# A two-layer perceiver block with int8-style feed-forward on one core: first loads reordered, last normalisation on POOL, float16 GELU inputs with an offset

## The reference

```python
x = x + xattn(layernorm(x), ctx, ctx, mask, Wq, Wk, Wv, Wo)   # 16 heads of 8, causal
x = x + attn(layernorm(x), Wq, Wk, Wv, Wo, Wd, Wuk, Wuv)       # 16 heads, scores clipped, times a decay
x = x + ffn(layernorm(x), w1, b1, w2, b2)
# ffn: each linear quantises its input and its weight by one scale for the whole tensor
s  = max(max(abs(v)), 1e-6) / 127
h  = gelu((round(x/sx) @ round(w1/sw).T + b1) * (sw*sx))
o  = (round(h/sh) @ round(w2/sw2).T + b2) * (sw2*sh)
```

## Time and profile before

| What | us |
|---|---|
| median of 3 runs | 324.59 |
| the profiled execution's own time | 324.61 |
| its span, first to last instruction | 322.8 |
| PE busy (share of the span) | 292.3 (91%) |
| DVE busy | 256.5 (79%) |
| ACT busy | 250.1 (77%) |
| POOL busy | 226.9 (70%) |
| mean granted PE clock | 0.974 |

### The profile page before, as it was taken

The page is one execution under the profiler, slowest core; times in us unless marked ns, Lnnn a source line. Parts: engine busy times, 40 slices in busy tenths (PEclk is TensorE's granted clock), DMA queues, the critical chain, the costliest instruction groups (busy, mean ns, idle before and its releaser), DMA issues.

```text
span 322.8 us, 13785 instructions
## 1 busy us (share of the span) xinstructions
PE 292.3 (91%) x5792; PEld 205.0 (64%) x5792; DVE 256.5 (79%) x561; ACT 250.1 (77%) x544; POOL 226.9 (70%) x176
## 2 busy tenths in 40 slices
PE   4796989999999999999999999999999998575884
PEld 3455757676767676867677777776667767321363
DVE  1486587899977887888788887878788998679883
ACT  3485795868687988787889898889877877499583
POOL 5177576874969697879999999999989970055000
PEclk9798999999999999999999999999999999759999
DMA  8999000000000000000000000000000000000027
GB/s 194 229 199 198 3 2 2 2 4 3 4 2 4 2 4 4 2 4 2 2 4 4 4 4 2 4 3 4 4 2 4 4 3 5 2 0 0 0 66 196
DMA packets 19102, 9.54 MB, mean 30 GB/s; under 512 B 5153, under 2 KB 18786, under 8 KB 19042
## 3 DMA queue, kind: packets, MB, share of 16 engines
q1 hardware_dynamic: 18322, 8.25, 12.0%
q10 hardware_dynamic: 720, 0.43, 0.6%
HBM read 6.57 MB, written 2.10 MB: 27 GB/s over the span
## 4 chain that ended last, share of the span: by engine, by line
PE 75%; ACT 14%; DVE 4%; issue 3%; DMA 1%; ACTq 1%; SPq 0%; DVEq 0%
PE ps L554 13%; PE ps L535 11%; PE ps L581 9%; PE ps L587 8%; PE ps L597 8%; PE ps L475 5%; ACT arena L860 4%; PE ps L459 4%; PE ps L468 4%; PE ps L552 4%; PE ps L566 3%; PE ps L645 2%; PE ps L441 2%; ACT arena L775 2%; DMA arena<-in_ctx 1%
## 5 line engine op out<-in xcount | busy, mean ns | idle before, releaser
L782 ACT ACTIVATE pt<-ps 128x512 f32<-128x512 f32 x128 | 75.9, 594 | 21.7 <-PE ps L554 20.7
L386 POOL TENSOR_TENSOR u<-u,mx 128x1024 f32<-128x1024 f32 x32 | 60.8, 1902 | 37.1 <-DVE mx L991 36.9
L378 POOL TENSOR_TENSOR ud<-u,con 128x1024 f32<-128x1024 f32 x31 | 73.5, 2372 | 1.9 <-DVE u L977 1.9
L972 DVE SCALAR_TENSOR_TENSOR u<-ps,rs,arena 128x1024 f32<-128x1024 f32 x32 | 41.0, 1282 | 20.3 <-PE ps L535 20.2
L535 PE MATMUL ps<-arena,qT 32*64 32x256 f32 x1024 | 44.2, 401 | 6.4 <-ACT arena L775 4.3
L977 DVE TENSOR_SCALAR u<-ps 128x1024 f32<-128x1024 f32 x32 | 39.0, 1220 | 12.5 <-PE ps L535 12.1
L581 PE MATMUL ps<-pt,vx 128*32 128x64 f32 x2048 | 41.0, 221 | 1.7 <-DVE oT L918 1.5
L581 PEld LDWEIGHTS ps<-pt,vx 128*32 128x32 f32 x2048 | 32.2, 110 | 14.8 <-issue 10.0
L587 PE MATMUL ps<-pt,con 128*32 128x128 f32 x1024 | 40.0, 275 | 0.0
L991 DVE TENSOR_REDUCE mx<-u 128x16 f32<-128x1024 f32 x32 | 38.7, 1210 | 0.1
L535 PEld LDWEIGHTS ps<-arena,qT 32*64 32x64 f32 x1024 | 14.9, 129 | 32.2 <-issue 22.5
(11 more groups left out here) (153 smaller groups left out, 568.2 us busy)
## 6 DMA issues: line engine op xcount, KB each, us to landing
out<-pt SPq DMA_DIRECT2D x8, 256.0 KB, 2.3
x<-in_x SPq DMA_DIRECT2D x4, 256.0 KB, 3.6
arena<-in_ctx SPq DMA_DIRECT2D x8, 128.0 KB, 4.1
x<-in_x SPq DMA_DIRECT2D x2, 512.0 KB, 7.0
arena<-in_ctx SPq DMA_DIRECT2D x4, 256.0 KB, 6.6
arena<-in_mask_BxS_if SPq DMA_DIRECT2D x2, 256.0 KB, 5.7
arena<-in_mask_BxS_if SPq DMA_DIRECT2D x4, 64.0 KB, 3.9
arena<-in_mask_BxS_if SPq DMA_DIRECT2D x2, 128.0 KB, 3.8
```

What stands on the lines that cost most here:

```text
L378: pool.tensor_tensor(dh, uh, decay.unsqueeze(1).to_broadcast([P, H, HALF]), ALU.mult)\
L386: pool.tensor_tensor(uh, uh, mx[:, n % 4, 0:count].unsqueeze(2).to_broadcast([P, count, HALF]), ALU.subtract)\
L782: act.activation(pt[:, n % 2, 4 * half:4 * half + 4].rearrange("p h n -> p (h n)"), ps[:, bank, :], ACT.Exp).then_inc(s["emptied"], 1)
L972: dve.scalar_tensor_tensor(by_head(u[:, n % UB]), sc, rs[:, 0, n:n + 1], mask[:, n].unsqueeze(1).to_broadcast([P, H, HALF]), ALU.mult, ALU ...
```

## The change

Six edits are in it.

Start: the context's first half is issued by ACT ahead of the identity, its second half by SP ahead of x; ACT's order is then identity, Wk, other constants, Wq, Wv. PE first runs 8 products on a zeroed tile `warm`, and the first pieces become c, x, k, cq, q.

Run-out: POOL normalises group 6 and three tiles of group 7; DVE normalises group 5 and tile 31 alone. The last tile's attention has a bank of its own (`num_den`), so it does not wait for the tile before it.

First maximum: its PE steps use bank 7 and stand ahead of the wait for the last copy. ACT loads the GELU table before its last two copies.

Up product: `x16` goes into PE as it is. `open_up` opens each pair of banks with w1 times -1536; the second pass into `xq` is gone. The first and the last GELU are halved.

Down product: POOL sums w2's four parts (`w2s`) in turns 30 and 31, so that `open_down` needs one product with `minus_off`, and the bias product moves into it, from the end of each group. Four groups are opened before the second maximum, the others between its steps and the first groups.

Rounding of the hidden values: ACT has groups 1, 3, 5, 7, POOL 2 and 6, DVE 0 (in halves) and 4.

```diff
-X_ACT = (1, 2, 3)
-X_POOL = 4
-H_ACT = (1, 2, 4, 5, 7)
-DVE_TAIL = (("a", 0), ("a", 3), ("f", 0), ("f", 1), ("a", 6)) + tuple(("f", g) for g in range(2, 8))
+WARM = 8
+X_ACT, X_DVE, X_POOL = (1,), (0, 2, 3), (4, 5, 6, 7)
+H_ACT, H_POOL = (1, 3, 5, 7), (2, 6)
+DVE_TAIL = (("a", 0), ("a", 4)) + tuple(("f", g) for g in range(8))
+GELUS = ((0, 0, 1), (0, 1, 2)) + tuple((k, 0, 2) for k in range(1, 15)) + ((15, 0, 1), (15, 1, 2))
...
-    pieces[-1] = [("x", 0), ("cq", 0), ("c", 0), ("q", 0), ("k", 0)]
+    pieces[-1] = [("c", 0), ("x", 0), ("k", 0), ("cq", 0), ("q", 0)]
...
+            def last_norm(g, tiles):
+
+                pool.wait_ge(RS[2], batch_of(2, tiles[-1]))
+                pool.wait_ge(s["filled"], gets_empty(("x3", g - 2)))
+                pool.wait_ge(s["amax_done"], g - 1)
+                for t in tiles:
+                    last = pool.tensor_scalar(xn3[:, g % 2, t % GT], x[:, t], mv[:, 2, t, 0:1], rs[:, 2, t:t + 1],
+                                              ALU.subtract, ALU.mult)
+                last.then_inc(s["xn3_pool"], 1)
...
+                if n == 30:
+                    pool.wait_ge(s["emptied"], gets_empty(("w2", 0)))
+                    pool.tensor_tensor(w2p[:, :, :], w2qT[:, 0:2], w2qT[:, 2:4], ALU.add).then_inc(s["w2_summed"], 1)
...
+            pool.wait_ge(s["hscale"], 2)
+            for g in H_POOL:
+                if g >= 6:
+                    pool.wait_ge(s["down_done"], g - 5)
+                pool.tensor_scalar(h16[g % 6], hidden[:, :, g * GT * P:(g + 1) * GT * P], scal[:, 19:20], ROUND16,
+                                   ALU.mult, ALU.add).then_inc(s["hr_done_pool"], 1)
...
+            def open_up(k):
+
+                for m in range(2):
+                    pe.matmul(ps[:, 2 * (k % 4) + m, :], w1qT[:, k % FC],
+                              minus_off[:, :].unsqueeze(1).to_broadcast([P, GT, P]), start=True, stop=False)
+
+            def open_down(g):
+
+                pe.matmul(ps[:, g, :], minus_off[:, :], w2s[:, :].unsqueeze(1).to_broadcast([P, GT, D]),
+                          start=True, stop=False)
+                pe.matmul(ps[:, g, :], ones_b[:, :], b2q[:, :].unsqueeze(1).to_broadcast([96, GT, D]),
+                          start=False, stop=False)
+
+            pe.wait_ge(s["warm_set"], 1)
+            for n in range(WARM):
+                pe.matmul(ps[:, OB, :], warm[:, 0:P], warm[:, :], start=True, stop=True)
...
+            pe.wait_ge(s["ared_local"], 1)
+            pe.transpose(ps[0:1, OB, 0:P], scal[:, 8:9], ident).then_inc(s["ared_row"], 1)
...
             pe.wait_ge(s["emptied"], max(fill.values()) + 1)
...
+            open_up(2)
+            pe.wait_ge(s["ascale"], 1)
+            open_up(3)
...
+            t0, t1 = LOADS[0]
+            act.dma_start(cx[0:HALF, t0:t1], ctx_t[0, 0:HALF, t0:t1]).then_inc(C_IN[0], 16)
             act.dma_start(con[:, 0:P], consts[:, 0:P]).then_inc(s["id_in"], 16)
```

More of the change, by code:

```diff
@@ L635, in _ @@
                 if k >= 4:
-                    pe.wait_ge(s["gelu_done"], k - 3)
+                    pe.wait_ge(s["gelu_done"], gelu_count(k - 4))
+                    open_up(k)
                 for m in range(2):
-                    n0 = (2 * pair + m) * GT * P
-                    last = pe.matmul(ps[:, 2 * (k % 4) + m, :], w1qT[:, c], xq[:, n0:n0 + GT * P],
-                                     start=True, stop=True)
-                last.then_inc(s["up_done"], 1)
-            def offset(g):
-                for c in range(FC):
-                    pe.matmul(ps[:, g, :], minus_off[:, :], w2qT[:, c].unsqueeze(1).to_broadcast([P, GT, D]),
-                              start=(c == 0), stop=False)
+                    g = 2 * pair + m
@@ L662, in _ @@
                 else:
-                    pe.wait_ge(s["hr_done_dve"], (1 if g == 0 else 1 + sum(e not in H_ACT for e in range(g + 1))))
+                    pe.wait_ge(s["hr_done_dve"], 1 if g == 0 else 3)
                 for i in range(GT):
@@ L833, in _ @@
                 weights(n)
+                if n == ROOT_TURN[2][-1]:
+                    act.activation(scal[:, 31:32], cst[:, 0:1], ACT.Gelu, bias=cst[:, 0:1])
                 if n == 24:
@@ L849, in _ @@
                             expand(j, h)
-            act.activation(scal[:, 31:32], cst[:, 0:1], ACT.Gelu, bias=cst[:, 0:1])
             act.wait_ge(s["ascale"], 2)
@@ L856, in _ @@
             act.wait_ge(s["ascale"], 4)
-            for k in range(16):
+            for k, m0, m1 in GELUS:
                 pair, c = divmod(k, FC)
-                act.wait_ge(s["up_done"], k + 1)
-                act.activation(hidden[:, c, pair * 1024:(pair + 1) * 1024],
-                               ps[:, 2 * (k % 4):2 * (k % 4) + 2, :].rearrange("p a n -> p (a n)"), ACT.Gelu,
+                act.wait_ge(s["up_done"], 2 * k + m1)
+                act.activation(hidden[:, c, pair * 1024 + m0 * 512:pair * 1024 + m1 * 512],
+                               ps[:, 2 * (k % 4) + m0:2 * (k % 4) + m1, :].rearrange("p a n -> p (a n)"), ACT.Gelu,
                                bias=b1s[:, c:c + 1], scale=scal[:, 12:13]).then_inc(s["gelu_done"], 1)
@@ L871, in _ @@
         def _(dve):
+            dve.memset(warm[:, :], 0.0).then_inc(s["warm_set"], 1)
             dve.memset(ones_row[:, :], 1.0)
@@ L1024, in _ @@
-            dve.wait_ge(s["amax_done"], NG)
+                    if g < BY_ACT and n == APPLY3[g] + 2:
+                        dve.wait_ge(s["xn3_ready"], 2 * g + 2)
+                        largest(g, 0, GT, g)
+                if n == APPLY3[5]:
+                    last_norm(5, range(20, 24))
+                    dve.wait_ge(s["xn3_last"], 1)
+                    largest(5, 0, GT, 5)
+                if n == NS - 1 + LAG_ADD[1]:
+                    dve.wait_ge(s["xn3_pool"], 1)
+                    largest(6, 0, GT, 6)
```

181 lines of the change are left out of this document (103 added, 78 removed).

## The result

The changed kernel takes 320.95 us in the median of 20 executions (319.35 to 325.23), the kernel before in the same rounds 324.56. The ratio is 0.9907 (95% interval 0.9882 to 0.9932): about 0.9%, or 3 us, faster; between the two medians lie 3.6. The ratio is of the fast executions alone, and leaves out the one of 325.23. The forecast was 318.9, inside a range that holds the time, but 2.05 us too low. The profiled execution took 320.3, with a span of 318.5 us where it was 322.8.

A forecast was written before the change was run, and what follows sets the result against it. PE, busy 91% of the span, was taken as the bound, so gains lay at the ends: 2.8 + 0 + 0 + 1.7 + 0 + 0.85 + 0.4 = 5.75, and 324.61 - 5.75 = 318.9 us, range 316.6 to 322.4.

The forecast's parts named there:

- Start: Loads and first pieces up to the early turns: context first and warm-up gain 2.8 us, the middle of 1.4 to 4.2.
- my lower bound of 1.4: Start: gain if PE stays at half clock, with the identity at about 4.8 us and first scores at 10.95.
- I let the gain pass on whole: After the start: ACT and PE set the pace of turns 1 to 10, so the full 2.8 us carries through.
- rival 3: Start gives only its lower bound, 1.4 us, with half clock down to 16 us: total 320.3 us; chance 0.14.
- Run-out: Last normalisations: POOL's seven tiles at 0.79 us end where DVE ended before, so 0, between +0.3 and -0.2.
- First maximum and first GELU: Not waiting for ACT's copy gains 0.65 us, reciprocal to first GELU 1.05; together 1.7 (1.3 to 2.1).
- GELU stage: DVE's 1.13 us a step stays the bound despite four PE products a step: 0, from -0.2 to +0.3.
- Second maximum: Fewer opening products let PE transpose the maximum at 305.2 us instead of 306.14: gain 0.85 (0.6 to 0.95).
- Second product: Down product after the second reciprocal: half clock for the first 4 to 5 us, gain 0.4, between -0.9 and 2.2.
- the rival: Second product: POOL and DVE exclude each other, DVE's second half waits to 3.6 us; total 321.8 us; chance 0.20.
- rival 1: Second product: the clock stays up, 1.8 us more gained, total 317.1 us; chance 0.10.
- Rival 4: Second product: POOL's rounding of 2048 strided columns runs slower, over 7.4 us making the kernel slower, up to about 335; chance 0.08.

The follow-up runs named there:

- number 7: Changed kernel, but of the last group POOL normalises two tiles and DVE two, instead of three and one: 321.57 us, ratio 0.992.
- Edits 4 and 5: Each on the changed kernel: 4 drops the 8 warm-up products, 322.22 us; 5 restores the old order of loads and first pieces, warm-up kept, 322.07 us.
- Edit 1: Changed kernel, but POOL's roundings of hidden values wait until DVE has done both halves of group 0: 320.72 us, ratio 0.9909.
- edit 2: Changed kernel, with 14 more opening products filling PE's rest before the second maximum: 320.80 us, ratio 0.9901.
- numbers 2, 3 and 7: 3 is the changed kernel with POOL's roundings delayed behind DVE's two halves and PE's rest before the second maximum filled: 320.32 us, ratio 0.9857.

## Why the prediction was right and wrong

The direction and the range were right; the sum was 2 us too favourable, and the measured time lies on the edge of what I had set for faster: the median is below 321.35, the ratio's 0.9% short of the 1%.

**Start (forecast 2.8, profile 3.32).** The size agrees, the parts don't. The first scores gained 0.92, less than my lower bound of 1.4: I took the identity's arrival from one issue (0.67), where PE's first transposes came 1.2 later than before (5.43 against 4.21), and left out that Wq, moved to the fifth issue of ACT, would be late for the query side. PE was also not slow all through this chain before, as I had read it: its key product took 1.07 at 9.24, where 1.13 is full pace and 2.07 half. Then 1.61 came from the first scores to the second, where before the clock was at half. The step that failed is "I let the gain pass on whole". Between tiles the fill repeats to 0.03 us in all traces but in four places, and one of these is chance: from tile 4 to 5 it takes 4.23, or 5.54 to 5.85 where half clock follows the wait of 2.6 us. Before, it took 5.84, after, 4.23, but so it was in six of eleven kernels with this wait, and long in five. So 1.6 of the pair's 4.46 belongs to the executions, not to the change. What is left is 2.06 up to tile 4 for this pair, and that hangs on the warm-up: against the one profile of the kernel before, tile 4 is 1.24 to 1.53 earlier in the seven kernels where it did not take hold, which is rival 3's lower bound of 1.4, and 2.06 to 2.65 in three of the four with the new order where it did (1.34 in number 7, with its spell). Edits 4 and 5, about 1.2 us each in the medians, fit in with this but do not show it.

**Run-out (0, profile -0.11).** Right, with the 0.79 a tile of the earlier trace rows: POOL ends with them, and DVE waits. Edit 7 shows that the split was not the best.

**First maximum and first GELU (1.7, profile 1.46).** The reciprocal gained more than the 0.65 for the copy (0.98). The first GELU gained less: I hid two of four openings behind DVE, but they began late and at half pace.

**GELU stage (0, profile -0.28).** At the edge of the range (0.2 to one side, 0.3 to the other). The halved GELUs let DVE start earlier and cost two more reductions; 19.66 is the same in nearly all kernels.

**Second maximum (0.85, profile 0.94).** Right for this execution. In numbers 4 and 7, whose clock was at half here, the stretch took 2.2 instead of 1.47, and the gain is 0.2.

**Second product (0.4, profile -0.87).** This is the failed term, 1.27 of it. I took half clock as the cause that decides, and gave the exclusion of POOL and DVE a chance of 0.20. It came: second half at 3.2 after the scale where the rival had 3.6 and my forecast 1.55. Its last step began at 12.6, where the rival had 14.2, the forecast 11.3, so the rival's mechanism was right and its price too high. The two causes are one chain, which I had priced apart: the exclusion makes PE rest, the rest brings half clock. Edit 1 removes the first cause and gains 0.94, edit 2 the other and gains nothing, both give 2.39, and without POOL's late group 3.2. With all of them the last step begins 9.35 after the scale, where rival 1, for the full clock, had worked out 9.45. Rival 4 fell: 2048 strided columns take POOL 1.97, below the 2.8 of four times 512.

Taken together: 2.06 for the start, 1.46 and 0.94 for the maxima, less 0.11, 0.28 and 0.87 is 3.2, near the 3.6 between the medians. An estimate, since how often each kernel has the 1.6, and how often its warm-up takes hold, is known from profiles alone.

## What to carry to other kernels

Two engines that are each early enough may still exclude each other: where POOL and DVE get the same kind of SBUF work released by one event, let POOL have the part that is due last and start it behind DVE's. Price a clock that falls and a wait that makes the engine rest as one chain, and test the two edits together: one alone can gain nothing. Where a profile pair differs by more than the medians, look for the stretches that take one of two values, and count in how many kernels each occurs.

## What the runs showed that was not expected

- With the new order, the first scores of the changed kernel and its variants stand between 10.86 and 12.27 us, and later tiles carry most of it. Two things go with it in the traces. In the four profiles at full pace (the changed kernel, numbers 2, 3 and 7) they stand 2.8 us behind the landing of Wq, which takes 4.5 to 5.1 us from its issue at 3.50. In the others the key product, at half pace, ends only at 9.2 to 9.5, and they stand at 11.99 or later. Why the warm-up takes hold in some executions only stays open.
- Up to about 9 us the granted clock reads 1.00 even where PE runs at half pace (transposes 1.08 in edit 4 at 5.67, 0.60 elsewhere); there I went by the durations.
- A rest of PE of 2.6 us is followed by half clock in some profiles and not in others, at the same place of the fill; filled, it was not in three profiles of three.
- All three kernels with products added before tile 4 pause at the same instruction near 272 us for 0.66 to 1.21 us, with no releaser; in no other profile does it pause there. What PE waits for there stays open.
